# A vision-tower kernel: two setup products and two small loads moved ahead of the first convolution

## The reference, cut to what matters

```python
gray  = einsum('bchw,c->bhw', x, (0.2989, 0.587, 0.114))
edges = conv(gray, scharr)                 # two 3x3 filters, SAME
h     = abs(edges).sum(axis=1) / 2         # (8, 256, 256): tokens x features
# attention, D = 256
Q, K, V = h @ Wq.T + bq, h @ Wk.T + bk, h @ Wv.T + bv
h = layernorm(h + softmax(causal(Q @ K.T / 16)) @ V)
# routed feed-forward, 8 experts, at most 320 tokens each
t = h.reshape(-1, 256)
probs = softmax(t @ Wr); idx = argmax(probs); pmax = max(probs)
y = relu(t @ W1[idx]) @ W2[idx]            # tokens over the cap keep t
h = layernorm(h + where(kept, y * pmax, t))
```

## Time and profile before

| | us |
|---|---|
| median of 3 runs | 244.31 (243.94 to 244.67) |
| the profiled execution | 243.94 |
| its span, first to last instruction | 242.2 |
| outside the span | 1.7 |
| PE busy | 228.4 (94%) |
| DVE busy | 183.6 (76%) |
| ACT busy | 150.6 (62%) |
| POOL busy | 91.8 (38%) |
| granted clock of PE, mean over the span | 0.991 |

### The profile page before, as it was taken

The page is one execution under the profiler, slowest core; times in us unless marked ns, Lnnn a source line. Parts: engine busy times, 40 slices in busy tenths (PEclk is TensorE's granted clock), DMA queues, the critical chain, the costliest instruction groups (busy, mean ns, idle before and its releaser), DMA issues.

```text
span 242.2 us, 4960 instructions
## 1 busy us (share of the span) xinstructions
PE 228.4 (94%) x1658; PEld 220.8 (91%) x1658; DVE 183.6 (76%) x549; ACT 150.6 (62%) x352; POOL 91.8 (38%) x168
## 2 busy tenths in 40 slices
PE   6999999999999999889999999999999999999940
PEld 5999999999999999658999999999999999999940
DVE  6878797788879798888666876868868688689650
ACT  5336567786878787466675676665766657665100
POOL 7001228484755656557100025230252302523472
PEclk9999999999999999999999999999999999999996
DMA  5916984074796020201799919155191550100100
GB/s 159 319 68 177 266 258 152 26 230 161 235 382 225 32 81 6 85 0 48 196 353 363 344 17 353 39 195 186 10 353 45 189 191 3 48 0 24 36 4 0
DMA packets 28234, 35.48 MB, mean 147 GB/s; under 512 B 2643, under 2 KB 25154, under 8 KB 28210
## 3 DMA queue, kind: packets, MB, share of 16 engines
q1 hardware_dynamic: 26050, 31.71, 40.7%
q0 software_dynamic: 1744, 3.47, 3.9%
q10 hardware_dynamic: 416, 0.00, 0.1%
HBM read 26.97 MB, written 9.47 MB: 150 GB/s over the span
## 4 chain that ended last, share of the span: by engine, by line
PE 83%; DVE 7%; issue 3%; POOL 3%; ACT 1%; POOLq 1%; DMA 0%; DVEq 0%; ACTq 0%
PE bank L1383 16%; PE bank L1385 16%; PE bank L1384 16%; PE bank L1454 14%; PE bank L1471 5%; PE bank L1508 5%; POOL out_dram L640 2%; PE bank L1524 2%; PE bank L1700 2%; PE bank L1648 2%; PE bank L1482 2%; DVE images L993 1%; PE bank L1526 1%; PE bank L1525 1%; POOL yrstd L664 1%
## 5 line engine op out<-in xcount | busy, mean ns | idle before, releaser
L1295 DVE SCALAR_TENSOR_TENSOR h_lo<-bank,h_hi 128x320 fp32r<-128x320 f32 x58 | 28.3, 490 | 25.1 <-ACT h_hi L905 22.1
L905 ACT ACTIVATE h_hi<-bank 128x320 fp32r<-128x320 f32 x58 | 25.4, 438 | 34.5 <-PE bank L1385 34.5
L1383 PE MATMUL bank<-einT_hi,w_hi 128*128 128x320 f32 x128 | 40.3, 315 | 0.2 <-DVE einT_lo L1287 0.2
L1385 PE MATMUL bank<-einT_hi,w_lo 128*128 128x320 f32 x128 | 39.5, 309 | 0.0
L1384 PE MATMUL bank<-einT_lo,w_hi 128*128 128x320 f32 x128 | 39.5, 309 | 0.0
L1044 DVE TENSOR_TENSOR w_lo<-w_raw,w_hi 128x1024 fp32r<-128x1024 f32 x32 | 38.9, 1215 | 0.0
L1383 PE MATMUL bank<-h_hi,w_hi 128*128 128x320 f32 x112 | 35.1, 313 | 0.0
L1385 PE MATMUL bank<-h_hi,w_lo 128*128 128x320 f32 x112 | 34.6, 309 | 0.0
L1384 PE MATMUL bank<-h_lo,w_hi 128*128 128x320 f32 x112 | 34.6, 309 | 0.0
L640 POOL DMA_INDIRECT out_dram<-tokens_mem,images x21 | 22.7, 1082 | 29.1 <-ACT tokens_mem L923 21.8
L821 ACT ACTIVATE w_hi<-w_raw 128x1024 fp32r<-128x1024 f32 x32 | 33.7, 1053 | 0.0
(11 more groups left out here) (236 smaller groups left out, 569.9 us busy)
## 6 DMA issues: line engine op xcount, KB each, us to landing
w_raw<-in_L_ffn_W_dram SPq DMA_DIRECT2D x16, 1024.0 KB, 7.6
images<-in_x_dram SPq DMA_DIRECT2D x7, 768.0 KB, 4.8
dispatched<-blank SPq DMA_DIRECT2D x4, 645.0 KB, 9.8
out_dram<-lone SPq DMA_DIRECT2D x8, 256.0 KB, 7.1
images<-dispatched SPq DMA_DIRECT2D x6, 258.0 KB, 5.8
images<-dispatched SPq DMA_DIRECT2D x3, 387.0 KB, 8.9
images<-in_x_dram SPq DMA_DIRECT2D x2, 384.0 KB, 4.8
out_dram<-tokens_mem,images POOLq DMA_INDIRECT x21, 2.9
```

The costliest lines, as they stand in the source:

```text
L905: act.activation(hidden_halves(n)[0], hidden_bank(n)[:, 0:CAP], ACT.Relu).then_inc(h_hi_ready, 1)
L1295: dve.scalar_tensor_tensor(lo, hidden_bank(n)[:, 0:CAP], 0.0, hi.bitcast(F32), ALU.max, ALU.subtract).then_inc(h_ready, 1)
L1383: pe.matmul(to, ah, bh, start=first, stop=False)
L1385: return pe.matmul(to, al, bh, start=False, stop=last)
```

## The change

It does five things.

1. PE makes two products of 128 columns on ones (into bank 3, overwritten by the key weights before it is read) before the taps are spread. The block of ones is written by DVE in two pieces of 256 columns with `one_row` between them; `still_ready` 1 releases the two products, `still_ready` 2 `keep_warm`.
2. `Wr` and `bvc` are loaded from POOL's queue, after the padding and before `avg`; `bvc` in one load with a semaphore of its own. SP issues three loads fewer.
3. The mean of the router's weights leaves `setup_values` and goes, with new products, into `setup_means`, which stands ahead of the first convolution: avg x `Wr` (2 products), bias x `Wr` (2), bias x avg (2).
4. The gate's constant is taken apart: `sum bv*Wr - 256 * mean(bv) * mean(Wr)`. `setup_gate` loses its two products for it; DVE gains a copy (`bias_mean`) and a multiplication (`mean_part`), and adds instead of copying into `const_gate`.
5. `setup_gate` and `residual_in` no longer wait for the `bvc` loads.

```diff
+            pool.dma_start(wr[:, :, :], Wr.rearrange("(c p) e -> p c e", p=P)).then_inc(wr_in, 16)
+            pool.dma_start(bvc[:, :], bv.rearrange("(c p) -> p c", p=P), allow_slow_non_contiguous=True
+                           ).then_inc(bvc_in, 16)
             settle()
             step(pool.memset(avg[:, :], 1.0 / D))
...
+            dve.memset(xT_hi[:, 0, 0].bitcast(F32), 1.0).then_inc(still_ready, 1)
             dve.memset(one_row[:, :], 1.0).then_inc(row_ready, 1)
-            dve.memset(xT_hi[:, 0].bitcast(F32), 1.0).then_inc(still_ready, 1)
+            dve.memset(xT_hi[:, 0, 1].bitcast(F32), 1.0).then_inc(still_ready, 1)
...
             dve.wait_ge(mean_done, 1)
             dve.wait_ge(wr_in, 16)
+            link(dve.tensor_copy(bias_mean[:, :], bank[5][:, CONST_OUT + E:CONST_OUT + E + 1]))
+            step(dve.tensor_scalar(mean_part[:, :], bank[5][:, 0:E], bias_mean[:, 0:1], -float(D), ALU.mult, ALU.mult))
...
-            step(dve.tensor_copy(const_gate[:, :], bank[5][:, BIAS_OUT + DC * E:BIAS_OUT + DC * E + E]))
+            step(dve.tensor_tensor(const_gate[:, :], mean_part[:, :], bank[5][:, CONST_OUT:CONST_OUT + E], ALU.add))
...
+            def setup_means():
+
+                pe.wait_ge(pool_const, 1)
                 pe.wait_ge(wr_in, 16)
                 for k in range(DC):
-                    ins = pe.matmul(bank[5][:, 0:E], avg[:, :], wr[:, k, :], start=(k == 0), stop=(k == DC - 1))
+                    pe.matmul(bank[5][:, 0:E], avg[:, :], wr[:, k, :], start=(k == 0), stop=(k == DC - 1))
+                pe.wait_ge(bvc_in, 16)
+                o = CONST_OUT
+                for k in range(DC):
+                    pe.matmul(bank[5][:, o:o + E], bvc[:, k:k + 1].broadcast_to([P, P]), wr[:, k, :],
+                              start=(k == 0), stop=(k == DC - 1))
+                for k in range(DC):
+                    ins = pe.matmul(bank[5][:, o + E:o + E + 1], bvc[:, k:k + 1].broadcast_to([P, P]), avg[:, 0:1],
+                                    start=(k == 0), stop=(k == DC - 1))
                 ins.then_inc(mean_done, 1)
...
+            pe.wait_ge(still_ready, 1)
+            for _ in range(2):
+                pe.matmul(bank[3][:, 0:P], xT_hi[:, 0, 0, 0:P], xT_hi[:, 0, 0, 0:P], start=True, stop=True)
             pe.wait_ge(row_ready, 1)
             pe.wait_ge(taps_in, 16)
...
-            pe.wait_ge(still_ready, 1)
+            pe.wait_ge(still_ready, 2)
             keep_warm(6)
             setup_keys()
             setup_biases()
+            setup_means()
```

More of the change, by code:

```diff
@@ L76, in vit_tower_kernel @@
         bank = [ctx.enter_context(nc.psum_tensor(f"bank{i}", [P, 512], F32)) for i in range(8)]
-        BIAS_OUT = 64
+        BIAS_OUT, CONST_OUT = 64, 16
         ident_wide = sb("ident_wide", [P, HALF + P])
@@ L110, in vit_tower_kernel @@
         const_gate = sb("const_gate", [P, E])
+        mean_part = sb("mean_part", [P, E])
+        bias_mean = sb("bias_mean", [P, 1])
         WCOLS = DC * F + FC * D
@@ L293, in vit_tower_kernel @@
         row_ready = sem("row_ready")
+        bvc_in = sem("bvc_in")
         late_values_ready = sem("late_values_ready")
@@ L430, in _ @@
             sp.dma_start(wv[:, :, :], Wv.rearrange("(c p) d -> p c d", p=P)).then_inc(wv_in, 16)
-            sp.dma_start(wr[:, :, :], Wr.rearrange("(c p) e -> p c e", p=P)).then_inc(wr_in, 16)
             load_picture(1)
-            for c in range(DC):
-                sp.dma_start(bvc[:, c:c + 1], bv[c * P:(c + 1) * P].rearrange("(p o) -> p o", o=1)
-                             ).then_inc(consts_in, 16)
             sp.dma_start(bvb[:, :], bv.rearrange("(o d) -> o d", o=1).broadcast_to([P, D])).then_inc(consts_in, 16)
@@ L1051, in residual_in @@
                 if b == 0 and s == 0:
-                    dve.wait_ge(consts_in, 48)
+                    dve.wait_ge(consts_in, 16)
                 ins = dve.tensor_tensor(xb[:, b % 2, s, :], bank[2][:, s * D:(s + 1) * D], bvb[:, :], ALU.add)
@@ L1408, in setup_values @@
             def setup_values():
-                pe.wait_ge(pool_const, 1)
                 pe.wait_ge(wv_in, 16)
@@ L1422, in setup_gate @@
                 pe.wait_ge(wr_centred, 1)
-                pe.wait_ge(consts_in, 48)
                 for c in range(DC):
@@ L1426, in setup_gate @@
                     for k in range(DC):
[L1427 to L1432, removed]
+                        ins = pe.matmul(bank[5][:, o:o + E], wv[:, k, c * P:(c + 1) * P], side[:, k, E:2 * E],
+                                        start=(k == 0), stop=(k == DC - 1))
                 ins.then_inc(setup_mm, 1)
```

## The result

| | before | after |
|---|---|---|
| median, us | 244.25 (243.93 to 244.84, 6 runs) | 247.78 (245.47 to 249.96, 6 runs) |
| ratio, 95% interval | | 1.0112 (1.0087 to 1.0137) |
| profiled execution, span | 243.94, 242.2 | 247.78, 246.0 |
| mean granted clock | 0.991 | 0.983 |

The kernel is 3.5 us slower by medians and 1.1% (2.7 us) by the ratio, which leaves out as slow the two longest after runs, 249.70 and 249.96 us, that the median holds. Forecast were +0.5 us and a range up to 245.5. Spread grew with the median: over the after runs the mean granted clock goes from 0.971, in one of the two longest, to 0.988, in the shortest.

A forecast was written before the change was run, and what follows sets the result against it. PE was taken as the bound after the setup, which ends at 17.44 us, with delays there passing to the end. Terms +0.97 - 0.35 + 0 + 0 - 0.1 = +0.52 us on the median 244.31 gave 244.8, range 244.0 to 245.5.

The forecast's parts named there:

- Six products ahead of the first convolution: Before the first convolution on PE: 12 added records at 0.105 us, 1.26 us, delaying its start by 0.97 us.
- The 0.29 us in which PE was ahead: Before the first convolution: PE's setup was 0.29 us ahead of the gray chain, so that much added work is free.
- The mean leaving the convolution: Between the first convolution's parts: 4 records go where PE is the bound, -0.35 us counted in full.
- The gate's constant at 0: Between convolution and image 0's values: 4 records, 0.44 us, leave PE, which then waits for DVE; cost 0.
- Rival D: The constant's 0.44 us does come off the path and the clock rises early; -0.24 us, 244.1; chance 0.11.
- The small products: Before the wait for the taps: no time cost, perhaps an earlier clock; bounds 0 and -0.42, taken as -0.1 us.
- rival B: The clock rises with PE's first product, gaining 0.42 us in the key weights; +0.2 us, 244.5; chance 0.20.
- The loads at 0: In the setup: `wr` and `bvc` from POOL's queue arrive before PE needs them, `bvc` 3.4 us after issue; cost 0.
- Rival C: `bvc` lands late and PE stands still before the first convolution; +1.7 us, 246.0; chance 0.11.
- DVE's additions: Before the first tokens: a copy and a multiplication, some 0.3 us, hidden in DVE's 0.60 us of idle time.
- A: The forecast: six products paid in front, the constant's gain lost waiting for DVE before the values; 244.8 us, chance 0.58.

The follow-up runs named there:

- e14: The changed kernel with its 24 narrow records in front made 120 columns wide, same products and loads; 245.57 us against 244.64 for the kernel before, +0.9.
- e9: The kernel before plus six float32 products of 120 columns behind the biases, results never read; 246.07 us against 244.74, +1.3.
- e5: The changed kernel with the means moved back behind the transposes of the value weights; 247.01 us against 244.73 for the kernel before, +2.3.
- e7: The changed kernel with three more products of 512 columns among the narrow ones; 247.56 us against 244.73 for the kernel before, +2.8.
- e3: The kernel before plus six float32 products of 8 columns behind the biases, results never read; 247.87 us against 244.28, +3.6.
- e16: The changed kernel with 120-column records in front and `bvc` loaded from ACT's queue; 245.48 us against 244.64 for the kernel before, +0.8.
- e1: The kernel before with only the two small products and the ones written in two pieces added; 244.21 us against 244.28, -0.1.
- e8: The kernel before with one product of 512 and one of 256 columns on ones ahead of the taps; 245.13 us against 244.73, +0.4.
- e2: The changed kernel without its two small products; 247.48 us against 244.28 for the kernel before, +3.2.
- e11: The kernel before with `bvc` alone loaded from POOL's queue, one load of 256 single elements; 245.42 us against 244.74, +0.7.

## Why the prediction was wrong

**The step that failed** is the first of the parts, "Six products ahead of the first convolution". It priced 12 records at 0.105 us and stopped there. The duration was nearly right (12 records from 10.05 to 11.39, 1.34 us and no wait; forecast 1.26, 1.05 to 1.32). What it put at nothing is what 24 records of 1 and 8 columns in a row do to PE's clock behind them: 3.4 us of the dense convolution at 1.2 GHz. That cost 1.6 us in the profiled execution (6.47 us of convolution against e14's 4.90), and over the runs, by e14 against the changed kernel, 2.6 us in the median and 1.7 us by the ratios. The forecast thought of the clock only as something that might rise sooner or later, never as something that can be lost again. No rival had the mechanism.

**The 0.29 us in which PE was ahead** existed in the profiled execution and hardly in the median one. In 18 profiles of these kernels the key weights, which nothing ahead of them changes but the clock's rise, took 2.04 to 3.61 us; in the kernel before it was 2.15, the fourth shortest. From 2.15 + 0.29 = 2.44 on PE is late by itself and each added record counts in full: e9 added 1.34 us of records and cost 1.3. The forecast itself guessed that a later rise puts the median above this execution, and still took the whole 0.29 off. Without this credit, and without the 0.1 us for an earlier clock, the sum is 1.26 - 0.35 = +0.91 us, and e14, the change without the fall, measured +0.9.

**The late rise in the profile after** is not the change's. Its key weights took 3.61 us, the longest of the 18; with the same products and loads ahead of them they took 2.10 in e14, 2.47 in e5 and 2.86 in e7. The +1.43 us in the table, of which the 0.29 took the first part, is what this one execution drew. That it still lies at the median is luck: its fall lasted 3.4 us, where e3's profile has one of 6.8.

**The mean leaving the convolution**, -0.35: right in kind, a little small. From the convolution's first record to the gate's first it took 5.40 us before, 4.90 in e14 and 4.91 in e16, so 0.5 went. With the measured 1.34 for the records in front that makes +0.84 for the work, and e16 measured +0.8.

**The gate's constant at 0**: right. From the gate's first record to the first value weight it took 3.16 us before and 3.15 after, with DVE's end 0.05 and 0.04 us ahead of the weight load. Rival D is out.

**The small products**: e1 measured -0.1 us with an interval across nothing, and e8, with more work at the same place, brought no earlier rise. Nothing supports the tenth of a microsecond taken for them, and rival B is out: PE started at 1.25 and 1.24, and the clock rose at 8.8 in the changed kernel and near 7.8 in e1, against 5.8 before with a start at 2.10. The statement of the Trainium skill, TensorE: Matmul & The Clock Gate, Part 1 (the HAM clock gate), that the watching runs freely fits these three.

**The loads at 0**: wrong by themselves. `bvc` landed 5.8 us after its issue where 3.4 was taken and 5.3 was the limit at the forecast's pace. It was issued earlier than feared, at 3.29, and the late clock hid the rest; in e2 and e14 PE waited 0.3 us for it. Rival C had the right tensor, but in the one bad execution that was profiled (e11) the harm was to other loads, `bqc` and image 0's second half. Alone the move of `bvc` is +0.7 us; in the changed kernel it adds nothing that the runs can tell. Whether VectorE locked GpSimd out, as rival C had it, no run tests: POOL's two issues took 0.94 and 0.75 us, no longer than its issues of the earlier trace rows.

**DVE's additions**: 0.15 and 0.23 us at 14.16 and 14.34, while DVE idled 2.6 us before the tokens. Right.

**The chances**: "slower" had 0.24, from rival C and the noise of A; that it came out slower by another mechanism is no merit of C. The bound of 245.5 came from terms of duration only.

## What to carry to other kernels

A product's price is its duration and what it does to the clock of the work behind it: before grouping small products on TensorE, look for the granted clock of the stretch that follows, and where a product's time does not depend on its columns, try a wider moving operand, which cost next to nothing here (12 records took 1.34 us with 8 columns and with 120) and kept the clock. A busy PE does not by itself keep its clock. A slack read from one execution near the fast end is not the median's slack. Before moving a load of single elements to an idle queue, measure that move alone.

## What the runs showed of the hardware that was not expected

- 24 float32 records of 1 and 8 columns over 2.6 us, PE busy throughout, were followed by a clock of 1.2 GHz for 3.4 us (changed kernel), in e3 by one from about 10.6 to 17.4 us. With the added records at 120 columns no run shows one (e9, e14, e16: 21 runs with mean clocks of 0.988 to 0.992). The fall did not come in every run of the narrow kernels: e3 had it in 4 of 6.
- The Trainium skill, TensorE: Matmul & The Clock Gate, HAM oscillation, tells of falls that come with PE's waits for a DMA. e11 has such a wait, of 2.6 us, but its fall comes 2.8 us after the wait's end and behind narrow records, so it does not show which of the two brought it. The changed kernel and e3 show it without any wait.
- The first rise came between 5.6 and 8.8 us in 18 profiles, by the length of the same eight records of key weights, whether PE had started at 1.25 or at 2.11. The granted clock's column reads 1.00 in the slow stretch too; only the spacing of the records tells.
- One load of 256 single elements (1 KB) issued from POOL, at 2.35 us in e11, cost 0.7 us by medians; beside it, in one of the two worst of 13 runs, a load of ACT's queue landed after 7.3 us, against 3.4 to 5.3 with all loads on their old queues; 8 KB of `Wr` in runs of 8 elements on the same queue cost nothing (+0.1, interval across nothing).
